# Attention inner step: the two halves of the weighing behind the second and the fourth pair of products

## The reference, cut to what matters

```
q, k, v = (src @ q_w, src @ k_w, src @ v_w), as [batch, head, token, 16]
scores  = q k^T / 4 * scale(q)
aw      = softmax(scores)
out     = aw v
```

## Time and profile before

| | |
|---|---|
| median of three runs | 2585.01 us |
| the profiled execution, its own time | 2593.07 us |
| its span in the trace | 2591.3 us |
| what lies around the span | 1.8 us |
| mean granted TensorE clock | 0.967 |
| busy: PE, DVE, ACT, POOL | 95%, 82%, 71%, 36% |
| first and last exponential's start | 788.5 us, 2233.8 us |

### The profile page before, as it was taken

One profiled execution on the slowest core, in us unless ns is written; L12 is line 12 of the kernel. 1 busy time (PEld: TensorE's weight loads), 2 busy tenths in 40 slices (PEclk: granted clock), 3 DMA queues, 4 the chain that ended last, 5 costly groups with the idle time before them and its releaser, 6 DMA issues. The chain is left out here.

```text
span 2591.3 us, 49197 instructions
## 1 busy us (share of the span) xinstructions
PE 2472.1 (95%) x18379; PEld 1251.9 (48%) x18379; DVE 2124.7 (82%) x4155; ACT 1828.8 (71%) x2336; POOL 939.5 (36%) x1059
## 2 busy tenths in 40 slices
PE   7999999999789999999999999999999999997996
PEld 5566665555444444444444444444444444474654
DVE  6778888988767898988898898898899996183877
ACT  4888878777215777777777787777787777662664
POOL 1777878888600212111121121112101010155664
PEclk8999999999877999999999999999999999997998
DMA  3322323332430402204031040040030000125883
GB/s 106 122 80 85 104 88 93 98 101 85 106 63 18 65 19 46 38 18 50 18 48 20 18 66 3 17 66 18 18 50 2 2 1 24 39 86 182 300 281 113
DMA packets 96463, 178.70 MB, mean 69 GB/s; under 512 B 19382, under 2 KB 66150, under 8 KB 88400
## 3 DMA queue, kind: packets, MB, share of 16 engines
q1 hardware_dynamic: 89488, 160.43, 24.6%
q0 software_dynamic: 6016, 14.49, 1.6%
q10 hardware_dynamic: 720, 0.62, 0.1%
HBM read 145.11 MB, written 31.21 MB: 68 GB/s over the span
## 5 line engine op out<-in xcount | busy, mean ns | idle before, releaser
L1670 DVE TENSOR_REDUCE max_part<-round_psum 128x1 f32<-128x512 f32 x2048 | 1294.1, 686 | 167.2 <-PE round_psum L1577 136.0
L1634 ACT ACTIVATE p_exp<-score_psum 128x1024 f32<-128x1024 f32 x1024 | 1046.4, 1024 | 299.3 <-PE score_psum L1562 299.3
L1562 PE MATMUL score_psum<-q_stack,k_stack 50*128 50x512 f32 x2048 | 843.3, 475 | 4.7 <-ACT p_exp L1634 2.8
L1577 PE MATMUL round_psum<-k_stack,q_stack 48*128 48x512 f32 x2048 | 784.6, 461 | 9.6 <-DVE max_part L1670 5.6
L1609 PE MATMUL pv_psum<-p_exp,values 128*17 128x256 f32 x8192 | 644.4, 387 | 2.4 <-ACT pv_out L1650 0.3
L1562 PEld LDWEIGHTS score_psum<-q_stack,k_stack 50*128 50x128 f32 x2048 | 365.5, 184 | 482.9 <-issue 436.0
L1577 PEld LDWEIGHTS round_psum<-k_stack,q_stack 48*128 48x128 f32 x2048 | 314.5, 187 | 76.5 <-DVE max_part L1670 40.9
L672 PE MATMUL rot<-tokens_t,w_in 128*128 128x512 f32 x576 | 271.7, 602 | 0.4 <-DVE x_conv L839 0.2
L1609 PEld LDWEIGHTS pv_psum<-p_exp,values 128*17 128x17 f32 x8192 | 136.1, 95 | 271.5 <-issue 257.6
L1713 POOL TENSOR_TENSOR rden<-pv_out,minus_one 128x16 f32<-128x16 f32 x31 | 90.0, 2903 | 427.9 <-ACT pv_out L1653 424.9
L1700 POOL CAST max_parts<-max_neg 128x16 fp32r<-128x16 f32 x32 | 6.3, 198 | 463.2 <-DVE max_neg L1676 441.3
(11 more groups left out here) (296 smaller groups left out, 3320.2 us busy)
## 6 DMA issues: line engine op xcount, KB each, us to landing
cum_rows_in<-cum_rows SPq DMA_DIRECT2D x64, 512.0 KB, 3.9
expert_w<-in_expert_w SPq DMA_DIRECT2D x24, 1028.0 KB
qk_rows<-split_then_gate SPq DMA_DIRECT2D x64, 256.0 KB, 4.0
tokens_t<-in_expert_w SPq DMA_DIRECT2D x15, 1028.0 KB
cum_pairs_in<-cum_rows SPq DMA_DIRECT2D x240, 64.0 KB, 2.8
q_stack<-qk_rows SPq DMA_DIRECT2D x42, 256.0 KB, 12.7
k_stack<-qk_rows SPq DMA_DIRECT2D x42, 256.0 KB, 15.8
token_rows<-tokens SPq DMA_DIRECT2D x12, 512.0 KB, 7.5
```

What stands on the lines that cost most here:

```text
L1562: m = nc.tensor.matmul(ebank[i // 2][:, i % 2, :], ks[rows, n % 2, plane, k * P:(k + 1) * P], qs[rows, n % 2, plane, q * BLK:(q + 1) * BLK ...
L1577: nc.tensor.matmul(bank[step][:, :], qs[rows, n % 2, plane, at:at + P], ks[rows, n % 2, plane, keys * BLK:(keys + 1) * BLK], start=True, s ...
L1634: nc.scalar.activation(pt[:, (k * 2 + pair) % 4, :, :], ebank[pair][:, :, :], ACT.Exp).then_inc(*exped.up(u, k, pair))
L1670: nc.vector.tensor_reduce(mx[:, c * HG + h, keys:keys + 1], bank[step][:, :], AX_X, ALU.max).then_inc(*maxed.up(u, k, i))
```

## The change

The two conditions that place the halves now look at the right member of a pair, not the left. ("max", 1) is the right member of the second pair and ("max", 3) that of the fourth.

```diff
                 if what != "max" and scoring:
                     yield what, u, k, i
-            if left == ("max", 0) and 0 <= t - 2 < total:
+            if right == ("max", 1) and 0 <= t - 2 < total:
                 yield "weigh", *divmod(t - 2, KT), 1
-            if left == ("max", 2) and 0 <= t - 1 < total:
+            if right == ("max", 3) and 0 <= t - 1 < total:
                 yield "weigh", *divmod(t - 1, KT), 0
         yield from due.get(t, [])
```

## The result

The changed kernel takes 2543.71 us (median of four runs, 2540.16 to 2556.50), the kernel before 2584.59 us on the same chip. The ratio is 0.9848 with a 95% interval of 0.9811 to 0.9884: faster by 1.5%, some 40 us. The forecast was 2529, the range 2508 to 2572. The profiled execution of the kernel after is one of its runs, 2541.72 us with a span of 2539.9; against the profiled execution before, its span is 51.4 us shorter: 0.5 us of that lie ahead of the first exponential, 43.7 between the first and the last E0, and 7.2 behind them, where the change alters hardly anything.

The account below looks back on a forecast made before the run. A latency loop through ACT and PE was taken to bound the step at 2.60 us. Terms -48.0, -20.5, -7.8, +28.2 and -7.7 (last stretch) sum to -55.8, taking the median from 2585.0 to 2529 us, range 2508 to 2572.

Parts of the forecast that it names:

- plain steps: Attention steps without item or copy: 331 of them, each from 2.595 to 2.45 us, together -48.0 us.
- rival A: Plain steps: signal or score slightly late each step, settling near 2.50 us; 2546, or 2567 without the items' gain; chance 0.18.
- W1 in the loop: Plain steps before: second weighing half stands inside the ACT and PE latency loop that bounds the step at 2.60 us.
- PE becomes the bound at 2.45: Plain steps after: latency loop falls to 2.41 us, 2.43 at most, under PE's own 2.45; DVE follows at 2.39.
- the margin of 0.04: Plain steps after: the gap by which the latency loop, 2.41 us, lies under PE's 2.45.
- m products' banks: nothing: Three banks of the m products, freed at least 0.2 us before use: no effect on time.
- The items: Steps with transposes or projections: pair group no longer cut, some 105 steps at 0.195 us, -20.5 us.
- The copy: Unit's end: pv_psum copy falls behind the exponential, PE stalls 1.05 us; k = 1 distances +28.2 us, k = 0 -7.8.
- B: Rival: the stall at the unit's end is hidden; 2501 us; chance 0.05.
- C: Rival: no net effect, plain-step gain (steps near 2.56) eaten by the copy; 2580 to 2590 us; chance 0.05.
- D: Rival: slower, pair groups don't close up, PE's step 2.645 us or at worst 2.84; 2626 us; chance 0.08.

Follow-up runs that it names:

- e2: Changed kernel with only the weighing half of step t-1 moved, the half of step t-2 back behind the first pair; 2570.80 us in one run.
- e1: Changed kernel with only the weighing half of step t-2 moved, the half of step t-1 back behind the third pair; 2669.67 us in one run.
- e5: Changed kernel with one signal per weighing half, at the fourth head, and both exponentials waiting for it; 2558.13 us, ratio 0.9880 to the kernel before.
- e9: Changed kernel with uneven weighing halves, 288 query columns for step t-1, 224 for step t-2; 2540.14 us, ratio 0.9811 to the kernel before.
- e4: Changed kernel with max_part in two buffers and the reduction over a unit's maxima five maxima later; 2535.62 us, ratio 0.9810 to the kernel before.
- e3: Changed kernel with the second weighing half of a unit's last step at the very start of step k = 1; 2514.37 us, ratio 0.9733 to before.
- e12: Changed kernel with the pv_psum copy put ahead of the step's first exponential in ScalarE's order only; 2523.24 us in one run.
- e7: Changed kernel with the edits of e3, e4 and e5 together; 2528.12 us, ratio 0.9757 to the kernel before.
- e8: Changed kernel run again, unchanged, to see its spread; 2548.08 us, ratio 0.9837 to the kernel before.
- e6: Changed kernel with the edits of e3 and e4 together; 2515.31 us, ratio 0.9696 to the kernel before.
- e10: Kernel of e6 with the uneven halves of e9; 2506.00 us, ratio 0.9659 to the kernel before.
- e11: Kernel of e6 once more, as neighbour of e10 on its chip; 2514.10 us, ratio 0.9702 to the kernel before.

## Why the prediction was right

The direction held, the range held the median, and most terms of the sum held step by step. What did not hold is which bound paces the plain steps. The gain was over-stated: 56 us against 41 in the medians and 44 in the attention of the two traces. The median, 2543.71 us, lies nearer to rival A's 2546 than to 2529; a range that reached over both could not tell them apart, the plain step does.

*W1 in the loop.* Right, and shown: with W0 alone moved the plain step stays at 2.594 (e2). But it is half of the reason. The forecast checked that s3 has slack after the change, but did not see that in the kernel before W0 stands in a second loop, over E1; with W1 alone moved that loop holds the step at 2.58 (e1). The change moves both halves, so the omission cost nothing here, by luck.

*PE becomes the bound at 2.45.* The size of the signal was wrong. I took 0.66 from the start of W1 to E0, with 0.68 as bound, from the last weighing and its copy. It is 0.72. So the loop is 2.466, not 2.41, and it stays just above TensorE's 2.449 (e5, e9). That is rival A in a mild form: the margin of 0.04 was not there, but s1's lateness of 0.02 upset no group, and the step settled at 2.47, not 2.50. Cost: 0.016 x 302 = 5 us. The estimate by the Trainium skill ("TensorE: Matmul & The Clock Gate", "The cost: per-tile semaphore tail"), a tail of 96 ns, which I had set against my bound, had the size right (0.094). The row that I used was of the very last weighing, with nothing behind it on TensorE, where the copy starts 0.05 behind the end. The trace of the kernel before had better ones. In each of the 31 steps k = 1 with a copy, it starts 0.72 behind W1, as here:

```profile
1574.72 0.63 PE L1609 MATMUL pv_psum<-p_exp,values 128*17 128x256 f32 x8
...
1575.44 0.58 ACT L1650 COPY pv_out<-pv_psum 128x512 f32<-128x512 f32 x1 [0.46 <-PE pv_psum L1609]
```

With 0.72 in place of 0.66 the forecast's own loop would have been 2.47, above its 2.45 for TensorE.

*"m products' banks: nothing".* Wrong in the step k = 12. I had left the reduction over the maxima out of VectorE's account of a step: with its waits it moves the next maximum by 0.42 us (due 2018.60, 0.04 behind its product's end as in the plain steps, seen at 2019.02), more than the 0.2 of slack that I had given the banks. It is the order that took the slack, not only the shorter step. From the end of that first maximum to the next product on its bank lie 0.74 us in the plain steps before (k = 12 takes 2.597), 0.36 after (2.65), and 0.12 in e2, where k = 12 takes 2.91 though the plain step is as long as before. Cost: 0.185 x 28 = 5 us, which e4 gives back. These two make some 10 of the 12 us between -55.8 and -43.7. About 3 us more were lost in two steps at a granted clock of 0.50 (below).

*The items.* Right in the main: turn_rows gains 0.19, turn_out 0.22 by the medians, from the uncut group, also without W1's move (e2).

*The copy.* Right in place and size. W0, due 0.67 behind the group that starts at 1948.84, comes 1.04 late, 1.05 forecast; the idle time of 0.97 (30.6 over all) is shorter, since the records of the products reach over their latency. Two small errors cancel in it: E0 came 0.06 later than forecast, and the copy ended 1.50 behind E0's start, not 1.57. e3 and e12 show that it is ScalarE's order.

*Rivals.* B is excluded by the idle time itself, C and D by the time; the uncut groups take 0.67 as forecast.

## What to carry to other kernels

When two engines hand a buffer back and forth, add up the loop before believing a busy share: the sum of latencies around E0, s1, W1, E0 gave the step to 0.01 us, and a stretch in which one engine has nothing to do, at the same period, is the proof that it isn't the bound. Add up every such loop, not only the longest: the one over E1 was only 0.1 us behind, and with it left in place the change would have been worth 0.01 us a step. When an experiment hits its number, look in its trace at what each instruction waited for; e1's number fitted the wrong theory. Work that doesn't belong in the loop goes outside it, but in an in-order list shared by all engines each move also moves what stands with it on the others: here one copy of 0.6 us behind an exponential cost 26 us. Once two bounds are within 1%, small things that had been hidden (a reduction, the place of a signal) cost their full size.

## What the runs showed of the hardware that I had not expected

With two signals for a half of the weighing, a waiting exponential (second head) and a waiting copy (fourth head) both start 94 ns behind the recorded end of its last matmul. With one signal, on the fourth head, the exponential starts 127 ns behind it (e5, e7), the copy 67 (e7). The copy behind the very last weighing starts some 50 ns behind its end.

The granted clock can fall to 1.2 GHz inside the attention. The profiled execution after shows it once, over some 7 us behind a stall at a unit's end, where two steps took 4.84 and 4.66 us. e8's, of the same kernel, shows it at another unit's end, the last, over 7 us; e5's shows 3 us at the same place, e4's 51 us from there on. e1's shows six, one of them 65 us long in the last stretch. Each of these falls begins within 4 us of the start of E0 in a step k = 1, so right behind such a stall. The profiles of the kernels without the stall or with a shorter one (the kernel before, e2, e3, e6, e7, e10, e11, e12) show none behind the slow start, nor does e9's, which has the stall. That the stall lets the clock fall is likely by this, but not shown. In the kernels whose runs spread widely the times go with the mean granted clock: the kernel before took 2575.20 us at 0.975 and 2589.03 at 0.967 beside e3, e10 2494.26 at 0.974 and 2508.76 at 0.967. Such spreads are as large as the smaller effects here, so those were read from the steps in the traces and not from the medians.
